# An attention stage's first round reordered, its spreading transfers cut into 16 rows, its maxima turned as bf16 parts

## What is computed

```
x = layernorm(x + self_attention(x))          # 16 heads of 8, causal, + power-law decay in the scores
x = layernorm(x + relu(Q2 K2^T) V2)           # cross attention with ctx (4, 512, 128), no softmax
x = layernorm(x + expert_ffn(x))              # argmax over 8 experts, 128 -> 512 -> 128
```

## Time and profile before

| | us |
|---|---|
| median of 3 runs | 210.08 (209.39 to 210.7) |
| profiled execution, its own time | 211.26 |
| its span, first to last instruction | 209.4 |
| PE busy in the span | 159.7 (76%) |
| VectorE busy | 122.4 (58%) |
| ScalarE busy | 70.9 (34%) |
| GpSimd busy | 35.6 (17%) |

### The profile page before, as it was taken

The page is one execution under the profiler, slowest core; times in us unless marked ns, Lnnn a source line. Parts: engine busy times, 40 slices in busy tenths (PEclk is TensorE's granted clock), DMA queues, the critical chain, the costliest instruction groups (busy, mean ns, idle before and its releaser), DMA issues.

```text
span 209.4 us, 3693 instructions
## 1 busy us (share of the span) xinstructions
PE 159.7 (76%) x1169; PEld 113.4 (54%) x1178; DVE 122.4 (58%) x316; ACT 70.9 (34%) x157; POOL 35.6 (17%) x49
## 2 busy tenths in 40 slices
PE   2853947979885899977997799948767949999810
PEld 2512524546653668654775566825633328999710
DVE  4620864778798765798864784425136204688850
ACT  3400000643154522356224472221200028677600
POOL 6300000300003000102031010501312100145462
PEclk9995555556996559995799856999995899999965
DMA  3469598337970372000000000000352457661000
GB/s 95 107 151 225 139 185 255 105 78 178 274 272 14 91 175 53 2 3 0 0 17 15 2 0 3 25 1 0 91 177 71 139 171 202 182 173 39 18 20 21
DMA packets 17968, 19.72 MB, mean 94 GB/s; under 512 B 2841, under 2 KB 13598, under 8 KB 17516
## 3 DMA queue, kind: packets, MB, share of 16 engines
q1 hardware_dynamic: 16324, 17.48, 31.4%
q0 software_dynamic: 752, 1.21, 1.9%
q10 hardware_dynamic: 872, 0.79, 1.6%
HBM read 14.48 MB, written 5.18 MB: 94 GB/s over the span
## 4 chain that ended last, share of the span: by engine, by line
PE 41%; DMA 14%; DVE 13%; SPq 11%; issue 11%; ACT 4%; POOL 3%; ACTq 1%; DVEq 0%; POOLq 0%
DMA kx<-k_dram 7%; PE ps_m L838 5%; PE ps_s L830 5%; PE ps_o L733 5%; PE ps_s L693 4%; PE ps_s L770 4%; DMA q_dram<-parts 3%; PE ps_s L717 3%; DVE es L927 3%; DVE mx L912 3%; PE ps_m L779 3%; PE ps_s L689 2%; SPq L340 2%; SPq L416 2%; POOL rstd L491 2%
## 5 line engine op out<-in xcount | busy, mean ns | idle before, releaser
L912 DVE TENSOR_REDUCE mx<-ps_s 128x4 f32<-128x1024 f32 (+1 forms) x24 | 28.9, 1221 | 16.7 <-PE ps_s L693 16.4
L927 DVE SCALAR_TENSOR_TENSOR es<-es,tab_sb 128x1024 f32<-128x1024 f32 x24 | 28.3, 1220 | 4.7 <-ACT es L577 4.6
L577 ACT ACTIVATE es<-ps_s 128x1024 f32<-128x1024 f32 x24 | 23.9, 1023 | 19.9 <-PE ps_s L717 19.8
L693 PE MATMUL ps_s<-kx,qx 72*128 72x256 bf16 (+1 forms) x128 | 23.7, 309 | 1.7 <-issue 1.2
L689 PE MATMUL ps_s<-maskb,identb 128*128 128x256 bf16 (+1 forms) x42 | 16.2, 386 | 8.5 <-DMA kx<-k_dram 8.4
L717 PE MATMUL ps_s<-qx,kx 74*128 74x128 bf16 (+1 forms) x128 | 20.4, 324 | 1.4 <-DVE mx L912 1.1
L491 POOL TENSOR_TENSOR rstd<-var,mhalf 128x2 f32<-128x2 f32 x8 | 7.4, 923 | 75.8 <-DVE var L867 75.8
L505 POOL DMA_INDIRECT out<-qx x13 | 12.8, 984 | 29.8 <-DVE qx L1038 25.7
L693 PEld LDWEIGHTS ps_s<-kx,qx 72*128 72x128 bf16 x128 | 14.7, 125 | 5.5 <-issue 3.3
L717 PEld LDWEIGHTS ps_s<-qx,kx 74*128 74x128 bf16 x128 | 13.8, 131 | 6.3 <-DVE mx L912 2.1
L648 PE MATMUL ps_o<-maskb,identb 128*128 128x512 bf16 x58 | 16.0, 421 | 0.3
(11 more groups left out here) (121 smaller groups left out, 219.7 us busy)
## 6 DMA issues: line engine op xcount, KB each, us to landing
es<-w1T SPq DMA_DIRECT2D x13, 256.0 KB, 3.2
w_sb<-w2T SPq DMA_DIRECT2D x8, 256.0 KB, 4.3
qx<-q_dram SPq DMA_DIRECT2D x9, 192.0 KB
kx<-k_dram SPq DMA_DIRECT2D x9, 192.0 KB
sorted_dram<-blank SPq DMA_DIRECT2D x8, 198.0 KB, 2.6
q_dram<-parts SPq DMA_DIRECT2D x20, 64.0 KB, 2.0
ctxT_sb<-ctxT SPq DMA_DIRECT2D x2, 512.0 KB, 7.9
qx<-sorted_dram SPq DMA_DIRECT2D x13, 66.0 KB, 2.7
```

The source lines that it names most:

```text
L577: act.activation(es[:, k % EBUF, :], sc[:, :], ACT.Exp, scale=float(DK) ** -0.5).then_inc(free, 1)
L693: mm = pe.matmul(o[:, j, :], qx[0:PAIRS, b, h, t * P:(t + 1) * P], kx[0:PAIRS, b, h, 0:keys], start=False, stop=(j == hs - 1), skip_group_ ...
L912: v.tensor_reduce(mx[:, b % 2, h0:h0 + n, t], sc[:, :].rearrange("p (h k) -> p h k", h=n), AX.X, ALU.max).then_inc(free, 1)
L927: v.scalar_tensor_tensor(out=e, in0=e, scalar=CEIL, in1=decay[:, 0:qs].unsqueeze(1).to_broadcast([P, nh, qs]), op0=ALU.min, op1=ALU.mult). ...
```

## The change

- `store`: Q's parts get the homes (0, 1), 2, 3 of four, K's (0, 3), 1, 2 of four. Four transfers for each, eight in all, as before.
- `spread_rows` in place of `spread_q` and `spread_k`: five transfers for each of Q and K, of 16 rows (the last of 8), where there were three of 24. The 72 rows hold the same nine pairs of parts in another order.
- Batch 0: ScalarE issues K's stores as well as its spreads. For other batches SP stores and spreads both, Q's stores and then K's.
- `shift`: VectorE splits minus the maxima into two bf16 parts (`mparts`) right after the half's last maximum. PE turns both in one bf16 matmul, ScalarE copies them to `mshift` of 32 partitions, and one transfer of 8 KB fills rows 72 and 73.
- The list: 14 L648 matmuls in place of 12 at the start, and 8 more behind the last shift of batch 0. Round 0 is written out as `FIRST`: three exponentials of batch 0, then `proj` of batch 2, and only then the first maximum of batch 1. Rounds 1 to 3 and `CHAIN` are as before.

```diff
+HOMES = ([(0, 1), (2,), (3,)], [(0, 3), (1,), (2,)])
+BLOCKS = ([0, 2, 2, 2, 0], [0, 0, 1, 2, 2])
...
-START = [("proj", 0, 0), ("proj", 1, 0), ("rouse", 0, 12), ("max", 0, 0), ("max", 0, 1), ("max", 0, 2),
-         ("max", 0, 3), ("shift", 0, 0), ("max", 0, 4), ("max", 0, 5), ("shift", 0, 1)]
+START = [("proj", 0, 0), ("proj", 1, 0), ("rouse", 0, 14), ("max", 0, 0), ("max", 0, 1), ("max", 0, 2),
+         ("max", 0, 3), ("shift", 0, 0), ("max", 0, 4), ("max", 0, 5), ("shift", 0, 1), ("rouse", 1, 8)]
+
+FIRST = [("exp", 0, 0), ("exp", 0, 1), ("exp", 0, 2), ("proj", 2, 0), ("max", 1, 0), ("exp", 0, 3), ("max", 1, 1),
+         ("exp", 0, 4), ("max", 1, 2), ("exp", 0, 5), ("pv", 0, 0), ("max", 1, 3), ("pv", 0, 1), ("shift", 1, 0),
+         ("max", 1, 4), ("max", 1, 5), ("ctx", 0, 0), ("shift", 1, 1)]
...
-    out = list(START)
-    for r in range(B):
-        out += [(kind, r + rel, u) for kind, rel, u in ROUND if 0 <= r + rel < B and (r > 0 or rel >= 0)]
+    out = START + FIRST
+    for r in range(1, B):
+        out += [(kind, r + rel, u) for kind, rel, u in ROUND if 0 <= r + rel < B]
...
+        def spread_rows(eng, b, w, half):
+
             n = H // halves(b)
+            heads = slice(half * n, (half + 1) * n)
+            eng.wait_ge(stored[b][w], 16 * (PARTS + 1))
+            for k, block in enumerate(BLOCKS[w]):
+                row, n = 2 * DK * k, 2 if k < len(BLOCKS[w]) - 1 else 1
+                eng.dma_start((qx, kx)[w][row:row + n * DK, b, heads, :],
+                              (q_dram, k_dram)[w][b, block:block + n, :, heads, :].rearrange("i d h t -> (i d) h t"))\
+                    .then_inc(spread[b][half], 16)
...
@@ SP, proj
+                    sides = range(2) if b else range(1)
+                    for w in sides:
+                        sp.wait_ge(first_part, 2 * b + w + 1)
+                        store(sp, b, w, 0)
+                    for w in sides:
+                        for i in range(1, PARTS):
+                            sp.wait_ge(parts_ready, 4 * b + 2 * w + i)
+                            store(sp, b, w, i)
                     for half in range(halves(b)):
+                        for w in sides:
+                            spread_rows(sp, b, w, half)
...
@@ ScalarE, proj
+                    if b == 0:
+                        act.wait_ge(first_part, 2)
+                        store(act, 0, 1, 0)
                     vp, free = filled(act, "m", piece, 2)
...
+                    if b == 0:
+                        for i in range(1, PARTS):
+                            act.wait_ge(parts_ready, 2 + i)
+                            store(act, 0, 1, i)
...
@@ ScalarE, shift
-                    act.activation(mshift[:, b % 2, u, 0, :], mt[0:H, 0:P], ACT.Copy, scale=-1.0).then_inc(mhi_ready, 1)
+                    act.activation(mshift[:, b % 2, u, :], mt[0:2 * H, 0:P], ACT.Copy).then_inc(free, 1)
...
-                    for i in range(2):
-                        act.dma_start(qx[PAIRS + i:PAIRS + i + 1, b, heads, :].rearrange("o h (t q) -> o (h t) q", t=NT),
-                                      mshift[:, b % 2, u, i, :]).then_inc(shifted[b][u], 16)
+                    act.dma_start(qx[PAIRS:PAIRS + 2, b, u * H // 2:(u + 1) * H // 2, :].rearrange("i h (t q) -> i (h t) q", t=NT),
+                                  mshift[:, b % 2, u, :]).then_inc(shifted[b][u], 16)
...
@@ PE, shift
-                    pe.transpose(mt[0:H, 0:P], mx[:, b % 2, u * H // 2:(u + 1) * H // 2, :].rearrange("p h t -> p (h t)"),
-                                 ident[:, :]).then_inc(full, 1)
+                    pe.matmul(mt[0:2 * H, 0:P], mparts[:, b % 2, u, :, :].rearrange("p i n -> p (i n)"), identb[:, :],
+                              start=True, stop=True).then_inc(full, 1)
...
@@ VectorE, max
+                    if u % (NU // 2) == NU // 2 - 1:
+                        for last in (u - 1, u):
+                            taken(v, "s", ("max", b, last))
...
+                        own(v.tensor_scalar(mparts[:, b % 2, half, 0, :], m, -1.0, None, ALU.mult))
+                        v.scalar_tensor_tensor(out=mparts[:, b % 2, half, 1, :], in0=m, scalar=-1.0, in1=mparts[:, b % 2, half, 0, :],
+                                               op0=ALU.mult, op1=ALU.subtract).then_inc(mparts_ready, 1)
```

More of the change, by code:

```diff
@@ L179, in decoder_kernel @@
         mx = sb("mx", [P, 2, H, NT])
-        mshift = sb("mshift", [H, 2, 2, 2, P], BF16)
+        mparts = sb("mparts", [P, 2, 2, 2, H], BF16)
+        mshift = sb("mshift", [2 * H, 2, 2, P], BF16)
         es = sb("es", [P, EBUF, 1024])
@@ L336, in store @@
         def store(eng, b, w, i):
-            homes = [k_dram[b, i]] if w else [q_dram[b, k] for k in range(i, 2 * PARTS - 1, PARTS)]
-            for home in homes:
-                eng.dma_start(home.rearrange("d h t -> h d t"), parts[:, b % 2, w, i, :]).then_inc(stored[b][w], 16)
+            for home in HOMES[w][i]:
+                eng.dma_start((q_dram, k_dram)[w][b, home].rearrange("d h t -> h d t"), parts[:, b % 2, w, i, :])\
+                    .then_inc(stored[b][w], 16)
         def halves(b):
             return 2 if b == 0 else 1
-        def head_group(b, half):
+        def spread_rows(eng, b, w, half):
             n = H // halves(b)
[L347 to L361, removed]
+            heads = slice(half * n, (half + 1) * n)
[5 more added lines that the diff above has]
+                    .then_inc(spread[b][half], 16)
         @block.sync
@@ L545, in _ @@
                                    .then_inc(free, 1)
-                if kind == "rouse":
-                    act.wait_ge(stored[b][1], 16 * PARTS)
+                    if b == 0:
+                        for i in range(1, PARTS):
+                            act.wait_ge(parts_ready, 2 + i)
+                            store(act, 0, 1, i)
+                if kind == "rouse" and b == 0:
                     for half in range(halves(b)):
-                        spread_k(act, b, half)
+                        spread_rows(act, b, 1, half)
                 if kind == "ctx":
@@ L908, in _ @@
                     t, h0, n = max_unit(u)
[L909 to L919 removed]
+                    ins = v.tensor_reduce(mx[:, b % 2, h0:h0 + n, t], sc[:, :].rearrange("p (h k) -> p h k", h=n), AX.X, ALU.max)
+                    ins.then_inc(free, 1)
+                    if u % (NU // 2) == NU // 2 - 1:
+                        for last in (u - 1, u):
+                            taken(v, "s", ("max", b, last))
+                        half = u // (NU // 2)
+                        if b >= 2:
+                            filled(v, "m", ("shift", b - 2, half))
+                        m = mx[:, b % 2, half * H // 2:(half + 1) * H // 2, :].rearrange("p h t -> p (h t)")
+                        own(v.tensor_scalar(mparts[:, b % 2, half, 0, :], m, -1.0, None, ALU.mult))
+                        v.scalar_tensor_tensor(out=mparts[:, b % 2, half, 1, :], in0=m, scalar=-1.0, in1=mparts[:, b % 2, half, 0, :],
+                                               op0=ALU.mult, op1=ALU.subtract).then_inc(mparts_ready, 1)
                 if kind == "exp":
```

49 lines of the change are left out of this document (12 added, 37 removed).

## The result

The changed kernel takes **213.56 us** (median of 4 runs, 212.27 to 214.86), the kernel before 209.88 measured beside it (4 runs). The ratio is 1.017 (1.010 to 1.024): slower by 3.7 us. A ratio leaves out runs that took over 1.5% more than the kernel's fastest, while a median is over all, so the two can differ by a few tenths of a per cent. The profiled execution took 213.54 us with a span of 211.8, which is 2.3 and 2.4 more than before.

The account below looks back on a forecast made before the run. Batch 2's first maximum, where compute and spread 2 meet, was to wait for slower spreads: +1.7, clock +1, w2 loads +0.7, shift -0.2, sum +3.2 us; 214.5 profiled, 213.3 us median, range 204.5 to 217.

Parts of the forecast that it names:

- What bounds it, and where the sum is to be made: Compute and batch 2's transfer chain end together at batch 2's first maximum, 56.49 us; the change touches little behind it.
- Spread rate: Q's and K's 16-row spreads: rate goes with partitions written, 109 GB/s instead of 164, +3.6 to +4.8 us a batch.
- The rival that goes by engines: Spread rate follows engines in use: 219 GB/s, spreads of 5.4 us, total 205.5 us; chance 0.24.
- First maximum 20.3, last shift 31.5: Batch 0: slower spreads less earlier stores move its first maximum from 19.1 to 20.3, its last shift from 29.69 to 31.5.
- First exponential 35.3: Batch 0: last shift at 31.5, plus 0.3, plus 3.5 for the dummies gives 35.3 in place of 37.11, -1.8 us.
- "Compute needs 19.4 us from the first exponential" and the idle 3.5 us: Up to batch 2's first maximum, compute needs 19.4 us from the first exponential, then stands idle 3.5 us for spread 2.
- The clock's +1 after an idle stretch: Behind 58.2 us: the granted clock falls after compute's idle 3.5 us, as after the 13 to 19 us gap; +1 us.
- the w2 loads' +0.7: w2 loads, now behind batch 2's transfers, queue near batch 1's shifts and batch 3's stores: 0 to +1.5, taken as +0.7.
- The dummies: Eight more ahead of the first exponential cost 1.8 us at full clock, 3.7 at half; any clock lift shortens only some 0.5.
- The signs that were named: About 110 GB/s at share near 1, 10 us spread-to-product, 2 to 4 us wait at batch 2, clock 1.00, shifts within 7 us.
- The shift, -0.2: One 8 KB transfer for two of 4 KB, with VectorE's split: together -1 to +0.3 us, taken as -0.2.
- The rival "the first shift is shut in": Batch 0's first shift waits behind SP's loads and slower spreads, first exponential at 39 to 40, total 217; chance 0.10.

Follow-up runs that it names:

- experiment 3: Changed kernel with Q's and K's transfers of 24 rows again: 213.5 us; kernel before with 16-row spreads and their stores, nothing else: 219.1 us.
- the best kernel: Changed kernel with 24-row transfers, no 8 dummies, spread 1 held until the first shift landed, GpSimd's residual addition held: 207.6 us, ratio 0.985.
- experiment 5: Changed kernel without 8 dummies, SP's late loads held until batch 0's last shift landed: 212.8 us; same with 24 rows and GpSimd's addition held: 209.7 us.
- experiment 7: Changed kernel with 24 rows, spread 1 and GpSimd's addition held, 8 dummies in place: 211.7 us, against 207.6 without the dummies.
- experiment 4: Kernel before with only the new order (batch 0's exponentials first): 215.2 us; changed kernel without the 8 dummies and with the old order: 217.7 us.
- experiment 1: Changed kernel with GpSimd's residual addition held back until batch 1's last shift: 213.0 us, ratio 1.012.
- experiment 2: Changed kernel without the eight dummies behind batch 0's last shift: 212.0 us median, two runs at 207.7 and 207.8, four at 211.8 to 212.8.
- experiment 6: Changed kernel without 8 dummies, spread 1 held until the first shift landed: 213.2 us; same with 24 rows and GpSimd's addition held: 207.6 us.
- GpSimd held: Changed kernel, its 8 dummies kept, with GpSimd's residual addition held back until batch 1's last shift: 213.0 us, ratio 1.012.
- 24 rows: Changed kernel, its 8 dummies kept, with Q's and K's transfers of 24 rows again: 213.5 us, ratio 1.008.

## Why the prediction was right, and where it wasn't

The time (213.3 forecast, 213.6 measured) and the mark on which it was built (batch 2's first maximum, 58.2 forecast, 58.05 measured) are right. The mechanism given for that mark is not: PE was to wait there for spread 2, and it did not wait for any transfer. By the prediction's own steps:

- **What bounds it, and where the sum is to be made: right.** Behind the first turn 148.9 to 152.4 us follow in all profiled executions. The list of landings left out one of 5.11 us, the store `q_dram<-parts` of batch 1 at 17.68, which stands ahead of spread 1; the later issue of spread 1 was charged all the same (+1.5, 0.9 measured).
- **Spread rate: right in direction, too low in size.** 109 GB/s forecast, 127 to 134 measured, at a share near 1. By the rate that is +2 us a spread, not +3.6 to +4.8. From first issue to landing, which is what the sum used, it was nearer: 13 us forecast for spread 2 and 12.3 measured, where there were 9.0; spread 1 took 12.2 for 9.7. Where both spreads are waited for the whole cost is nearer 4 a batch (experiment 3). The Trainium skill, SBUF — State Buffer, "Door 1: the DMA port swizzle", gives 104 GB/s for partitions 0 to 15. No row here shows so little; but the fall of the rate with the rows written at a time agrees with it. The rival that goes by engines (219 GB/s) is refuted: 16 of 16 engines are busy and the rate is lower.
- **First maximum 20.3, last shift 31.5: both too late,** 18.38 and 29.62 were measured, as the slower spreads cost less than the earlier stores and that rate allowed.
- **First exponential 35.3: too late by 2.1,** by the same amount, since the dummies' 3.5 us (3.4 measured) were right.
- **"Compute needs 19.4 us from the first exponential" and the idle 3.5 us: the step that failed.** 19.4 was the distance in the old order, with batch 1's first three maxima done before it. The new order puts them behind the first exponential. In the kernel before they take from 32.54 to 37.11, 4.6 us. So about 24.0 was to be expected, and 24.8 was measured (33.23 to 58.05); 24.7 without dummies, 23.9 in the best kernel. PE had no 3.5 us to idle, and batch 2 waited for compute, not for spread 2.
- **Why the number came out all the same:** the first exponential was 2.1 us too late in the forecast, and compute after it 5.4 too short: 54.7 by its own numbers, 58.05 measured. Spread 2, put at 57.9, landed at 56.50. The forecast 58.2 was spread 2's time, and compute, taken to be 3.5 us ahead of it, ended there by luck. The two chains still end within 1.6 us of each other, as they did before the change, and in experiment 5 the spread was the later one. The median flatters the sum a little: for the profiled execution 214.5 was forecast and 213.5 measured (+3.2 and +2.3), while the medians grew by 3.7.
- **The clock's +1 after an idle stretch, the w2 loads' +0.7:** behind the first turn the span grew by 0.6, not 1.7. Neither was isolated.
- **The dummies:** taken as costing 3.5 us and lifting nothing that counts; that held. Their price was hidden in the forecast, for batch 2 was to wait for a transfer anyway. In truth they are 3.7 to 4.2 us where the first shift has landed (experiment 7), and by the medians some 1.5 in the changed kernel itself, where without them it sometimes hasn't.
- **The signs that were named:** the wait of 2 to 4 us for `kx` or `qx` at batch 2's first maximum did not come, nor a clock at 1.00 right behind the dummies in this execution. 10 us or more from first spread issue to PE's first product did (44.21 to 58.28). The first shift landed within 7 us (6.8), the second did not (30.24 to 38.41, 8.2 us).
- **The shift, -0.2 (bounds -1 to +0.3):** alone it measured +0.6%, or +0.4 to +2.0 us by the interval, so outside the bounds.
- **The rival "the first shift is shut in"** did not decide in the changed kernel: the shift landed at 32.24, 6.8 us after its issue, and the dummies covered it up to 33.2. It is real in other kernels: 31.1, 33.1 and 34.4 in experiments 5, 4 and 3. It was the spread ahead of it that shut it in and not, as the rival said, SP's loads alone.

The whole account, then: 16-row spreads, with their stores, cost 8.7 us alone (shown). The new order hides most of that (217.7 to 212.0, shown), at the price of exposing the shift's transfer. The dummies cover this wait, and cost some 4 us where there is none (shown). Compute behind the first exponential, which the order does not shorten but lengthens by three maxima, sets batch 2's start in the changed kernel (no DMA wait there, and it stayed where it was when spread 2 landed 1.7 us earlier, experiment 1). That it moved with the first exponential in experiment 2 proves nothing by itself, for the spreads follow the exponentials too. With the old 24-row transfers, no dummies, the shift ahead of spread 1 and GpSimd out of the way, the kernel with the new order is 2.8 us under the kernel before; how much of that is the order's, no run tells.

What stays open: the slower four runs of the kernel without dummies were not profiled. That their first shift was caught behind spread 1 is argued from experiments 5 and 6, where a shift issued 0.9 us later landed at 31.1, and where, at 24 rows, the hold brought the runs within 1.7 us; it is not shown. Those four runs also had a lower mean granted clock (0.819 to 0.833, against 0.845 and 0.846 in the two faster), which can be a result of the wait or a cause of its own. Where the new shift loses its 1.2 us in the kernel before is open too.

## What to carry to other kernels

When a change moves work from before a mark to behind it, the distance from that mark measured in the old order is no longer the distance: add what moved. A small transfer on which an engine waits belongs ahead of a bulk transfer in time of issue, not merely on another queue; here a wait of SP on the small one went with 207.6 us instead of 209.7 at 24 rows, and gained nothing at 16, where the bulk transfer then came too late. Dummy work ahead of the path's next real instruction has to be paid in full unless that instruction waits for something else, so ask what a faster clock behind it would shorten: where it came back here, VectorE was busy all the time at either clock (experiment 7).

## What the hardware showed

- **A transfer of 8 KB issued on another engine's queue behind a spread of 1.18 MB landed 6.0 to 8.7 us after its issue, in one execution 4.2 us (experiment 2), and 2.0 us after it with nothing ahead.** The Trainium skill, DMA: Bandwidth & Descriptors, "Issuing engines are not separate DMA queues", says that transfers of all issuing engines run on the same 16 DMA engines; the rows of experiments 5 and 6 agree, with the price.
- **More DMA engines, less rate:** 16 rows keep all engines busy at 131 GB/s, 24 rows three quarters of them at 164 to 172. The two kinds also differ in the number of transfers (five and three a tensor) and in the rows at which they start; no run separates these.
- **VectorE was blocked for 2.06 us by a GpSimd addition** (2.49 against 0.43), in an operation with two SBUF inputs. The Trainium skill, SBUF — State Buffer, "Who interferes with whom", says that such an operation contends with GpSimd's reads; the trace agrees. In the kernel before the same addition (at 36.28 us) fell beside maxima, whose only input is in PSUM, and nothing was blocked. It cost PE 2.6 us in one kernel (experiment 6, 16 rows) and nothing measurable in another (experiment 1), by what VectorE would have waited for next.
- **The granted clock came back to 1.00 for 3.4 us behind the eight dummies in three of the four profiled executions that have them**: from 35.2 us (GpSimd held), 33.6 (24 rows) and 30.8 (experiment 7). In the changed kernel's own it stayed at 0.50 (1.2 GHz). None of the six variants of it without the dummies shows such a stretch between 23 and 46 us; the kernel before with the new order has one, from 26.0 to 29.4, so it can come without them. GpSimd held:

```profile
36.00:38.00 2.00, 1.05 (x7) 0.59 (x4) 2.00 (x3) 2.00 (x4) 0.00 (x0) 1.00 1.14 329
```

- **The lasting rise came later, and not by the dummies.** First the changed kernel, then the same without dummies:

```profile
52.00:54.00 2.00, 2.00 (x28) 1.24 (x27) 1.28 (x2) 0.27 (x1) 0.00 (x0) 0.92 0.91 119
```

```profile
46.00:48.00 2.00, 1.94 (x29) 1.03 (x26) 1.51 (x2) 0.16 (x1) 0.00 (x0) 0.80 1.08 131
```

In both it rose with batch 0's attention products and batch 1's last maxima, wherever these stood; in experiments 6 and 7 (24 rows) it rose at 47.6 without dummies and at 47.9 with them. Why it came back behind the dummies in three executions and not in the fourth, no run here tells.
